# A graph-attention and expert kernel: tokens sorted by expert on the chip, in place of every expert for every token

## What is computed

```python
# attention: x += softmax(leaky_relu(f1[:, None] + f2[None, :]) + mask(adj)) @ layernorm(x)
# experts, on xf = layernorm(x):
logits = xf @ gate_w + gate_b
probs = jax.nn.softmax(logits, axis=-1)
top2_vals, top2_idx = jax.lax.top_k(probs, 2)
cw = jnp.zeros((N, Ee)).at[jnp.arange(N)[:, None], top2_idx].add(top2_vals)
def step(acc, params):
    w1, bb1, w2, bb2, we = params
    h = jax.nn.gelu(xf @ w1 + bb1, approximate=False)
    y = h @ w2 + bb2
    return (acc + we[:, None] * y, None)
```

## Time and profile before

| | us |
|---|---|
| three runs | 512.33, 508.79, 513.11 (median 512.33) |
| profiled execution, first to last instruction | 509.6 |
| TensorE busy | 471.5 (93%) |
| VectorE busy | 425.4 (83%) |
| ScalarE busy | 234.3 (46%) |
| GpSimd busy | 46.7 (9%) |
| last attention matmul issued | 319.4 |

### The profile page before, as it was taken

How to read it: one execution, slowest core, us unless ns; L and a number is a source line. 1 busy time by engine, 2 the same in 40 slices (tenths; PEclk the granted TensorE clock), 3 DMA queues, 4 the chain that set the end, 5 groups by cost and what they waited for, 6 DMA issues and landing times.

```text
span 509.6 us, 5787 instructions
## 1 busy us (share of the span) xinstructions
PE 471.5 (93%) x1712; PEld 221.2 (43%) x1712; DVE 425.4 (83%) x726; ACT 234.3 (46%) x362; POOL 46.7 (9%) x98
## 2 busy tenths in 40 slices
PE   2799999799979999899998999798999999999996
PEld 2773434245335444454444534343434444444442
DVE  0447679798998998989989897579899898988985
ACT  1539810113200200102001124689888888988883
POOL 8903202001010020020000000100000000000000
PEclk9859999999989999999999999999999999999999
DMA  6999999999809639389000000423443346445520
GB/s 193 183 106 105 105 106 202 168 163 90 76 2 97 66 30 105 31 77 88 0 0 0 1 0 21 153 84 82 104 82 113 124 118 122 84 103 112 126 50 22
DMA packets 35042, 44.49 MB, mean 87 GB/s; under 512 B 2592, under 2 KB 24528, under 8 KB 34768
## 3 DMA queue, kind: packets, MB, share of 16 engines
q0 software_dynamic: 17920, 18.88, 37.4%
q1 hardware_dynamic: 16288, 25.37, 19.7%
q10 hardware_dynamic: 816, 0.03, 0.1%
HBM read 92.38 MB, written 2.23 MB: 186 GB/s over the span
## 4 chain that ended last, share of the span: by engine, by line
PE 55%; DVE 23%; issue 7%; DMA 7%; ACT 6%; DVEq 1%; SPq 0%; ACTq 0%
PE bank L1044 20%; DVE c L828 11%; PE bank L1089 4%; PE bank L1091 4%; PE bank L1090 4%; DMA x<-in_x 4%; PE bank L1078 4%; PE bank L1080 4%; PE bank L1079 4%; DMA share<-in_L_gnn_inlayer 2%; DVE maskT L640 2%; PE bank L966 2%; ACT mask L567 2%; DVE xs L714 2%; DVE maskT L891 2%
## 5 line engine op out<-in xcount | busy, mean ns | idle before, releaser
L1044 PE MATMUL bank<-c,Y 128*128 128x512 f32 x512 | 232.9, 603 | 8.9 <-DVE c L828 8.3
L828 DVE SCALAR_TENSOR_TENSOR c<-g_row,r_col,maskT 128x512 f32<-128x512 f32 (+1 forms) x256 | 182.1, 744 | 17.8 <-PE bank L1044 14.0
L1044 PEld LDWEIGHTS bank<-c,Y 128*128 128x128 f32 x512 | 93.1, 191 | 132.7 <-issue 75.5
L885 DVE TENSOR_TENSOR mask<-mask,share 128x1024 f32<-128x1024 f32 x64 | 78.2, 1223 | 21.0 <-ACT mask L567 18.5
L567 ACT ACTIVATE mask<-bank,b1T 128x512 f32<-128x512 f32 x128 | 83.8, 688 | 22.8 <-PE bank L1080 21.2
L891 DVE TENSOR_TENSOR maskT<-mask,maskT 128x1024 f16<-128x1024 f32 x64 | 78.4, 1225 | 0.0
L574 ACT ACTIVATE maskT<-mask 128x1024 f16<-128x1024 f32 x64 | 67.4, 1053 | 3.2 <-DVE mask L885 3.1
L1089 PE MATMUL bank<-maskT,w2h 128*128 128x512 f16 x128 | 49.1, 383 | 5.7 <-DVE maskT L891 5.2
L1090 PE MATMUL bank<-maskT,w2h 128*128 128x512 f16 x128 | 49.0, 383 | 0.0
L1091 PE MATMUL bank<-maskT,w2l 128*128 128x512 f16 x128 | 49.0, 383 | 0.0
L1078 PE MATMUL bank<-share,w1h 128*128 (+1 forms) x128 | 48.5, 379 | 0.0
(11 more groups left out here) (145 smaller groups left out, 355.4 us busy)
## 6 DMA issues: line engine op xcount, KB each, us to landing
share<-shares SPq DMA_DIRECT2D x16, 1024.0 KB, 8.3
mask<-in_adj POOLq DMA_DIRECT2D x24, 512.0 KB, 17.2
mask<-in_adj POOLq DMA_DIRECT2D x32, 128.0 KB, 25.6
share<-in_L_gnn_inlayer SPq DMA_DIRECT2D x2, 1024.0 KB, 10.0
share<-in_x POOLq DMA_DIRECT2D x8, 256.0 KB, 12.2
out<-c SPq DMA_DIRECT2D x8, 256.0 KB, 3.8
share<-in_L_ffn_W SPq DMA_DIRECT2D x1, 1024.0 KB, 21.6
W_sb<-in_L_gnn_W SPq DMA_DIRECT2D x1, 64.0 KB, 2.0
```

Of the source, the lines that this page charges most:

```text
L828: dve.scalar_tensor_tensor(c[:, k % CR].rearrange("p (s i) -> p s i", i=32), g_row[:, bass.ds(s * ST, ST)].rearrange("p (s i) -> p s i", i ...
L885: dve.tensor_tensor(hw[:, e % 2], h[:, e % 2], wb[:, e].unsqueeze(1).to_broadcast([P, FC, ST]), ALU.mult).then_inc(hw_done, 1)
L1044: mm(bank[:, par, :], Y[:, k], c[:, k % CR], start=(k == 0), stop=(k == NK - 1)).then_inc(c_used, 1)
```

## The change

The experts are computed for a token's two experts alone. After routing, each choice of a token gets a slot: its rank among the rows of its expert, found by TensorE from the 0/1 matrix of choices (`rank`), plus the start of the expert, rounded up to 256. GpSimd writes the token's row (two float16 halves and a row number, 528 bytes) to that slot of a buffer in memory, 128 rows with each indexed transfer (`place_row`). This is done in two groups, 20 chunks (27 tiles of 256 slots) and 12 chunks (19 tiles); the first group's slots are made in supertile 6. For each of the 46 tiles SyncE loads the sorted rows in order (`load_tile`, a ring of 12), TensorE transposes them, runs the expert's two layers with an expert number read into a register, VectorE copies the result out, and GpSimd writes it back by row number, two indexed transfers a tile (`place_choice`, 12 result buffers). SyncE loads both results of a supertile and VectorE adds them to x with their shares (`combine`); it stores five supertiles among the last tiles and three after them. The unused slots are first cleared to rows that nobody reads (`fill`).

Beside it: the loops over supertiles are written out; the low halves are made by GpSimd (`low_rows`) for six supertiles and by VectorE for two; `post_b` transposes float16 halves after step 24, `post_c` follows after step 27; `b2` is loaded behind the weights, as 2 x 1024 values; lists of shares are gone. The diff's core:

```diff
 # SyncE
             sp.dma_start(w2raw, W2.rearrange("e (c f) d -> f (e c) d", c=FC)).then_inc(w_in, 16)
+            for i in range(2):
+                sp.dma_start(b2_raw[i:i + 1], b2.rearrange("(a e) d -> a (e d)", a=1)).then_inc(b2_in, 16)
+            def load_tile(t):
+                if t == 0 or t == TILES[0]:
+                    for s_in in sorted_in[t > 0]:
+                        sp.wait_ge(s_in, 16 * (GROUP[t > 0][1] - GROUP[t > 0][0]))
...
+                if t >= XR:
+                    sp.wait_ge(y_out[(t - XR) % YR], 16 * TP * ((t - XR) // YR + 1))
+                sp.dma_start(xt[:, t % XR].rearrange("p s w -> p (s w)"),
+                             sorted_x[TW * t:TW * t + TW].rearrange("(p s) w -> p (s w)", s=TP)).then_inc(xt_in[t % XR], 16)
 # GpSimd
+            for s in range(4, NS):
+                low_rows(s - 4)
+                load_adj(s, s % 2)
...
+            pool.wait_ge(filled, 64)
+            pool.wait_ge(slot_ready, 1)
+            for n in range(*GROUP[0]):
+                place_row(0, 0, n)
+            second_ids()
+            for n in range(*GROUP[0]):
+                place_row(0, 1, n)
...
+            pool.wait_ge(xld_ready, 2)
+            pool.wait_ge(c_used, NS * NK)
+            pool.tensor_copy(rows_2, rows[:, GROUP[1][0]:NK]).then_inc(ids_moved, 1)
...
+            for t in range(NT):
+                if t == SECOND:
+                    pool.wait_ge(slot_ready, 2)
+                    for n in range(*GROUP[1]):
+                        place_row(1, 0, n)
+                        place_row(1, 1, n)
+                place_choice(t)
 # place_row and place_choice; second_ids waits for the first 20 to land and adds 4096 to the row numbers
+                pool.indirect_dma_start(out=sorted_x, out_offset=bass.IndirectOffsetOnAxis(ap=slot_i[:, v, n:n + 1].bitcast(U32), axis=0),
+                                        in_=rows_2[:, n - GROUP[1][0]] if (r, v) == (1, 1) else rows[:, n],
+                                        in_offset=None).then_inc(sorted_in[r][v], 16)
+                for i in range(TP):
+                    pool.indirect_dma_start(out=choice_y, out_offset=bass.IndirectOffsetOnAxis(ap=xt_id[:, t % XR, i, D:D + 1].bitcast(U32), axis=0),
+                                            in_=y_sb[:, t % YR, i], in_offset=None).then_inc(y_out[t % YR], 16)
 # VectorE, for each tile (LAG is 2); combine(s, 0) and combine(s, 1) stand at tiles 37 to 41 and at the end
+            for t in range(NT):
+                high(t)
+                if t >= LAG:
+                    evict(t - LAG)
+                low(t)
...
+                if t == STD + 2:
+                    post_c(NS - 1)
 # TensorE, for each tile
+                experts.append(pe.value_load(expert[0:1, t:t + 1], min_val=0, max_val=E - 1))
...
+                if t + 1 < NT:
+                    turn_x(t + 1)
+                ffn1(t)
+                if t >= LAG:
+                    ffn2(t - LAG)
+                    for i in range(TP):
+                        mm(dst[:, i], hh[:, r, f, P * i:P * i + P], w2, start=(f == 0 and i == 0), stop=False)
+                        mm(dst[:, i, 0:D], hl[:, r, f, P * i:P * i + P], w2h, start=False, stop=False)
```

More of the change, by code:

```diff
@@ L154, in gnn_moe_kernel @@
[L154 to L158, removed]
+        b2hl = sb("b2hl", [2, E * D], F16)
+        upper = sb("upper", [2, 1])
+        lower = sb("lower", [2, 1])
@@ L358, in _ @@
+            for t in range(NT):
+                load_tile(t)
+                if COMBINE <= t < COMBINE + HEAD:
+                    load_choices(t - COMBINE, TILES[0])
+                if t >= NT - 3:
+                    store(t - NT + 3)
+            for s in range(3, HEAD):
+                store(s)
+            for s in range(HEAD, NS):
+                load_choices(s, NT)
+            for s in range(HEAD, NS):
+                store(s)
+            sp.wait_ge(out_done, 16 * NS)
         @block.gpsimd
@@ L426, in _, with low_rows @@
[L426 to L429, removed]
+            pool.tensor_scalar(b2_raw, b2_raw, lower[:], None, ALU.mult)
+            pool.tensor_scalar(b2hl[:], b2hl[:], upper[:], None, ALU.mult).then_inc(S_step, 1)
+            pool.wait_ge(S_step, 4)
+            pool.tensor_tensor(b2hl[:], b2_raw, b2hl[:], ALU.add).then_inc(b2_split, 1)
+            def low_rows(s):
+                pool.wait_ge(xtok_ready, s + 1)
+                pool.tensor_tensor(rows16[:, s * TS:s * TS + TS, D:2 * D], xn2[:], rows16[:, s * TS:s * TS + TS, 0:D],
+                                   ALU.subtract).then_inc(xlp_ready, 1)
@@ L440, in _ @@
                      (b1_sb[:], b1.rearrange("e (c f) -> (e c) f", c=FC)),
[L441 removed]
+                     ]
             for n, (dst, src) in enumerate(small):
@@ L814, in _, with supertile @@
             BN = (12, 13, 17, 18)
             TURNS = (15, 20, 24, 28)
-            def supertile(s, par, n, first=False, last=False):
-                router = route_b(*ROUTE[0])
+            routers = [route_b(r) for r in range(2)]
+            def supertile(s, first=False, last=False):
+                par = s % 2
                 for k in range(NK):
@@ L845, in supertile @@
                         post_b(s - 1, BN.index(k))
-                    if not first and k == 25:
+                    if last and k == 23:
                         post_c(s - 1)
@@ L940, in _ @@
-            for st in range(PEELED):
-                experts(st)
-            with dve.Fori(PEELED, NS) as st:
-                experts(st)
-            low(NS * E - 1, E - 1)
-            add_out(NS - 1)
+            for s in range(NS):
+                supertile(s, first=(s == 0), last=(s == NS - 1))
+            post_0(NS - 1)
+            post_a(NS - 1)
+            post_sum(NS - 1)
+            post_b(NS - 1, 0)
+            dve.wait_ge(post_step, (NS - 1) * POST + 1)
+            post_b(NS - 1, 1)
@@ L948, in _ @@
+            for t in range(NT - LAG, NT):
+                evict(t)
+            for s in range(HEAD, NS):
+                combine(s, 0)
+                if s > HEAD:
+                    combine(s - 1, 1)
+            combine(NS - 1, 1)
         @block.tensor
@@ L1133 @@
+            for t in range(NT - LAG, NT):
+                ffn2(t)
 _INS = ["x", "adj", "L0_gnn_inlayer2", "L0_gnn_W", "L0_gnn_b", "L0_gnn_w1", "L0_gnn_b1", "L0_gnn_w2", "L0_gnn_b2",
```

711 lines of the change are left out of this document (382 added, 329 removed).

## The result

The changed kernel takes 561.5 us (median of four runs, 561.2 to 563.0); the kernel before took 511.4 beside it. The ratio is 1.099, 95% interval 1.095 to 1.104: 9.9% slower, where I had forecast 1.9%. The direction was right and the time lies in the range (485 to 592), but 40 us are missing from my sum.

What follows compares the result with a forecast made beforehand. TensorE was taken to bound both halves before the change. Experts start at 347, second group's rows are loaded at 442, 20 tiles end at 503, tail to 519, plus 2.7: 522 us, 1.9% slower; range 485 to 592.

Steps and rivals of the forecast that it cites:

- The wait in the second supertile: TensorE waits for GpSimd's low_rows, queued behind the split of late-loaded b2: +15 us, bounds 0 and +35.
- The six instructions: GpSimd's split of b2 on 2 x 1024 values before low_rows: 8.3 us for all six, taken as 9.
- The end of attention: TensorE's last attention matmul, ending at 320 us before the change, was to end at 333.
- Slots of the first group: Known at step 30 of the seventh supertile, a little over one supertile before attention ends: 300 us.
- The tail: After the last results land: first result loads, VectorE's adds for the last three supertiles and the last store, 15.8 us.
- The price c: GpSimd's time for one indexed transfer of 128 rows: 1.0 us, between 0.6 and 1.55.
- T = 454 + 68c: The forecast's own sum for the whole kernel, with c entering 68 times: 522 us at c = 1.0.
- T = 357 + 156c: Rival sum where GpSimd becomes the bound: above the other from c = 1.1, 591 us at c = 1.5; chance 0.20.
- The rival's own sign: In the new profile, GpSimd's issues standing end to end through the whole expert phase: forecast wrong on the slow side.
- The late copy: GpSimd's copy ahead of placing results needs VectorE's step at tile 4: results start 29 us after the experts begin.
- The second group: Expert phase: slots at 408 us, GpSimd there at 413, rows loaded at 442, TensorE standing from about tile 26.
- The clock: Rival: TensorE's clock falls to half speed in the expert phase with its longer waits, 566 us; chance 0.08.

Runs made afterwards that it cites:

- the other run: A third indexed transfer of 128 rows of 16 bytes added for every tile of the changed kernel: 617.8 us.

## Why the prediction was right and wrong

- *The wait in the second supertile*: +15 forecast, 18.9 measured, ended by GpSimd's subtraction as said. The load landed at 113.2 for 114.5. The six instructions took 14.0 us instead of 9: the cast (1.03) and the two with two inputs (2.11 each) came out as priced, the three `TENSOR_SCALAR` took about 2.8 each, where I had put a copy's 1.06. Taken away, the wait gives back 17.7 us.
- *The end of attention*: the last matmul was to end at 333, it starts at 332.9. *Slots of the first group*: 300, measured 302.3. *The tail*: 15.8 behind a landing of 2.5, so 18.3 from the last issue; measured 15.6 (543.9 to 559.5).
- *The price c, the step that failed*: 1.0 forecast. The busy time was well estimated, 0.64 + 0.38 = 1.02 against 0.97. But c entered the sum as the distance from one issue to the next, and 0.30 us lie between two of them, which the plain issues did not show. The distance is 1.27. The start of the experts shows it first: 40 issues of 1.0 were to bring it at 347, and it came at 367.3, since 39 of them stood 1.27 or more apart and the first took 7.69.
- *Which sum decides*: at 1.27 it is no longer T = 454 + 68c (540) but the rival's, T = 357 + 156c: 555. The crossing was put at c = 1.1, and the rival had a chance of 0.20. That only 6.4 us remain to 561.5 is in part luck. Against that sum at 1.27 the slots came 2.3 us late, the first 40 issues, their landing and the first load took 7.0 more (6.7 of it in the first issue), and the 116 issues took 6.4 more, 1.33 apart; the results began 22.9 us after the experts instead of 29, and the end was 3.4 shorter. The rival's own sign was in the list: issues end to end through the whole expert phase.
- *The argument against that rival*, that for most tiles 2c would have to exceed 2.4 us, fell with c: 2 x 1.27 is 2.54. It also used too slow a tile, for the second group's take 1.85 where nothing holds them up.
- *The late copy* of the second group's rows was seen (results 29 us after the experts begin; measured 23, from 367.3 to 390.2). Not seen was that the last supertile waits for the first tile's rows; the run that undoes it is 11.8 us faster.
- *The second group*: slots at 408, measured 422.8 (L932), late by the late start: from the start it was 55.5 us, forecast 61. GpSimd got to them at 438.3, 15.5 us later instead of 5, since it still had results to place. TensorE's second stand came, 36.1 us, ended by a load at 472.1 instead of 442. For the tiles behind it, the adds of 1.8 and 0.7 make 2.5 us and not the 2.65 of the sum, 3 us in all. In the run with half of the results, where GpSimd's row no longer bounds throughout, the time was 530.7.
- *The clock*: granted 0.56 and 0.50 while TensorE stood, as the earlier trace rows suggested. The run with a third of a tile's matmuls left out took the same time, so what the lower clock adds to the tiles costs nothing so long as GpSimd's row is the bound.

So the change removes TensorE work, 78 us of it, and hangs the end on 156 issues of 1.27 us, 198 us that only 31 us of attention cover.

## What to carry to other kernels

When work becomes sparse, count the instructions that move it and multiply by the distance between two of them, not by the length of one bar; look for the pause in front. An engine that was 9% busy becomes the bound if every row of the result passes through its queue one issue after another. Price a queue's rival sums at the upper bounds of that one number before trusting the likelier of them; here 0.3 us an issue lie between a sum of 522 us and one of 555.

## What was not expected of the hardware

- An indexed transfer's issue on GpSimd costs 0.97 us undisturbed with 128 indices of 16, 512 or 528 bytes, and 0.30 us more before the next one. With 16 indices the mean is 0.895, beside 1.002 for 128 in the other run. What fills the 0.30 us is not shown.
- The first such issue behind the slots took 7.5 to 8.0 us in the changed kernel and in ten of the twelve experiments; a memset ahead of it or a stop of VectorE changes that, and no run showed why. On a page of the Trainium skill, SBUF — State Buffer, section Who interferes with whom, VectorE instructions with two operands in SBUF contend with GpSimd instructions that read it. That fits ends of 0.98 and 0.1 us after VectorE's pauses began in the runs with the memset and with the wait; the issues that passed later beside the same VectorE instructions do not follow from it.
- The price of a GpSimd instruction did not follow its number of inputs: on 2 x 1024 values a cast took 1.03 us, one with two inputs 2.11 and a `TENSOR_SCALAR` with one 2.8.
